# Sequence 0's lead-in in one block, and the third layer's three norms inside its mix: a four-layer transformer on one core

## The reference, cut to what matters

```python
xln = _ln(x, ln1_w, ln1_b)                 # x is already layer 3's normed input here
att_out = sigmoid(xln @ Wr) * (xln @ Wv) @ Wo
rwkv_state = xln @ Ws
x = x + att_out
h = _ln(x, ln2_w, ln2_b)                   # routed on, further down
```

## Time and profile before

| | us |
|---|---|
| median of 3 runs (2219.67, 2219.96, 2226.17) | 2219.96 |
| the profiled execution, as timed | 2215.92 |
| its span, first to last instruction | 2214.2 |
| first attention scores begin, from the span's start | 50.58 |
| layer 3, first norm of ffn to the start of norm 3b | 1578.14 to 1634.32 |
| `chunk_inputs3`, first projection to last spill | 1681.6 to 1817.8 |

### The profile page before, as it was taken

One profiled execution on the slowest core, in us unless ns is written; L12 is line 12 of the kernel. 1 busy time (PEld: TensorE's weight loads), 2 busy tenths in 40 slices (PEclk: granted clock), 3 DMA queues, 4 the chain that ended last, 5 costly groups with the idle time before them and its releaser, 6 DMA issues. The chain is left out here.

```text
span 2214.2 us, 45686 instructions
## 1 busy us (share of the span) xinstructions
PE 1846.9 (83%) x17745; PEld 992.8 (45%) x17751; DVE 1612.4 (73%) x2720; ACT 1216.6 (55%) x2472; POOL 674.7 (30%) x755
## 2 busy tenths in 40 slices
PE   2888877866647999999988889999788979887987
PEld 1222221443221335963233357776564434555755
DVE  5999999785779997569963955554756649876367
ACT  2999999532333886258866245556433620221475
POOL 1112120321675542124444633330214620000160
PEclk7899899987876999999989989999789979998986
DMA  8422430100551532733321122212001341430310
GB/s 280 91 58 58 97 77 1 77 19 6 136 190 30 123 59 79 209 76 68 50 32 45 43 65 66 65 53 80 11 23 46 123 142 75 141 94 13 119 53 34
DMA packets 156703, 171.87 MB, mean 78 GB/s; under 512 B 55468, under 2 KB 125174, under 8 KB 156482
## 3 DMA queue, kind: packets, MB, share of 16 engines
q1 hardware_dynamic: 142904, 144.03, 23.8%
q0 software_dynamic: 13584, 24.92, 4.5%
HBM read 95.58 MB, written 77.28 MB: 78 GB/s over the span
## 5 line engine op out<-in xcount | busy, mean ns | idle before, releaser
L464 ACT ACTIVATE a_E<-a_scores,a_nmax 128x512 f32<-128x512 f32 x512 | 343.2, 814 | 14.2 <-DVE a_nmax L397 13.2
L1057 ACT ACTIVATE a_E<-a_scores 128x512 f32<-128x512 f32 x512 | 273.8, 601 | 97.2 <-PE a_scores L1092 92.1
L397 DVE TENSOR_REDUCE a_nmax<-a_scores 128x2 f32<-128x1024 f32 x256 | 302.5, 1217 | 20.8 <-PE a_scores L479 17.1
L961 DVE TENSOR_REDUCE a_nmax<-a_first 128x2 f32<-128x1024 f32 x256 | 295.6, 1217 | 15.2 <-PE a_first L1082 14.0
L479 PE MATMUL a_scores<-a_Vh,a_Kh 48*128 48x512 bf16 x512 | 108.2, 421 | 96.0 <-ACT a_E L464 71.9
L1082 PE MATMUL a_first<-a_Kh,a_Qh 48*128 48x512 bf16 x512 | 148.2, 417 | 36.8 <-PEq L51 20.1
L492 PE MATMUL a_turn<-a_E,a_QS 128*32 128x256 f32 x2048 | 174.1, 417 | 2.3 <-DVE a_QS L407 1.8
L464 ACT ACTIVATION_READ_ACCUMULATOR a_E<-a_scores,a_nmax 128x1 f32 x512 | 167.0, 334 | 0.0
L1092 PE MATMUL a_scores<-a_Qh,a_Kh 51*128 51x512 bf16 x512 | 161.0, 396 | 5.1 <-PEq L51 1.9
L1114 PE MATMUL a_out<-a_E,a_V 128*32 128x256 f32 x2048 | 162.7, 398 | 0.0
L2193 POOL DMA_INDIRECT outs<-f_ye,f_row_at x80 | 78.2, 977 | 144.7 <-ACT f_ye L2314 112.5
(11 more groups left out here) (599 smaller groups left out, 4422.6 us busy)
## 6 DMA issues: line engine op xcount, KB each, us to landing
f_up<-in_L_up SPq DMA_DIRECT2D x32, 256.0 KB, 3.3
a_Kh<-a_rows_k SPq DMA_DIRECT2D x16, 384.0 KB, 6.5
a_Vh<-a_rows_v SPq DMA_DIRECT2D x16, 384.0 KB, 9.9
a_Qh<-a_rows_q SPq DMA_DIRECT2D x32, 192.0 KB, 4.9
a_Kh<-a_rows_k SPq DMA_DIRECT2D x32, 192.0 KB, 5.7
slots<-empty SPq DMA_DIRECT2D x8, 645.0 KB, 6.4
f_xe<-slots SPq DMA_DIRECT2D x40, 129.0 KB, 2.1
outs<-zeros SPq DMA_DIRECT2D x8, 512.0 KB, 4.7
```

Of the source, the lines that this page charges most:

```text
L397: v.tensor_reduce(nmax[:, rd % 2, r1, :, q], bank(b, u)[:], AX.X, ALU.max, negate=True).then_inc(S["max_ready"], 1)
L464: m = a.activation(E[:, u % NE, x], bank(b, u)[:, x], ACT.Exp, bias=nmax[:, rd % 2, r1, x, q:q + 1], accum_out=Z[:, rd % 2, r1, x, q:q + 1])
L961: v.tensor_reduce(out, slot_bank(n)[:], AX.X, ALU.max, negate=True).then_inc(S["slot_read"], 1)
L1057: a.activation(E[:, u % NE, x], ps_s[n % 3][:], ACT.Exp, scale=SCALE).then_inc(S["exp_ready"], 1)
```

## The change

Five things. (1) The loading block, `layer_norm` "0" and the first block of `attention0` become one block. x comes in five parts (the first is one sequence); sequence 0 alone is normed, turned, projected and split; the other sequences' norms and turns follow. ACT asks for the seven small weights at its very start. K and V are handled apart, in halves of 512 columns; ACT makes all three casts. SP writes K's parts, ACT V's; the rows are read back in eight smaller DMAs per tensor half, those of the first head group first (`load_first_rows`), and the first units wait only for these. (2) Sequence 1's K|V stays in f32; POOL makes its parts at the start of the attention block. (3) The twelve fills, `ln_cols` and the weights of ffn 0 are asked for inside the attention block, after the row loads of sequences 1 to 6. `QS` is zeroed by POOL in the first block, and the Exp table is loaded there. (4) In `ffn3`, norms 3 and 3a are merged into the mix: both roots come from the spreads of X, DVE and POOL each normalise four row groups per sequence (four for `rows`, four for XN), PE turns both; `ps_s`, `ps_o` and the two turning banks are one bank each. (5) In `chunk_inputs3`, ACT takes v's sigmoid after the gate, and POOL puts out two tiles ahead of the wait for it instead of one ahead and one behind.

The diff, cut to its core:

```diff
+def load_first_rows(eng, rows, dst, sem, first):
+
+    for x in range(2):
+        src = rows.rearrange("(x q i d) t s -> x (d t) q i s", x=2, q=2, d=HD)[x]
+        heads = dst[64 * x:64 * x + HD * TERMS].rearrange("p (q i) s -> p q i s", q=2)
+        for q in range(2):
+            if first:
+                eng.dma_start(heads[:, q, 0], src[:, q, 0]).then_inc(sem, 16)
+            else:
+                eng.dma_start(heads[:, q, 1:4], src[:, q, 1:4]).then_inc(sem, 16)
...
+                    load_x(0)
+                    sp.dma_start(g.ident[:], w["identity"]).then_inc(S["ident_loaded"], 16)
+                    for n in range(1, 5):
+                        load_x(n)
+                    sp.wait_ge(S["k_parts"], 1)
+                    spill_left(sp, rows_k[0], parts[:, :, 0:T], S["k_spilled"])
+                    sp.wait_ge(S["k_spilled"], NSP // 2)
+                    load_first_rows(sp, rows_k[0], Kh[:, 0], rows_first[0], True)
+                    sp.wait_ge(S["v_spilled"], NSP // 2)
+                    load_first_rows(sp, rows_v[0], Vh[:, 0], rows_first[1], True)
+                    load_first_rows(sp, rows_k[0], Kh[:, 0], rows_rest[0], False)
+                    load_first_rows(sp, rows_v[0], Vh[:, 0], rows_rest[1], False)
...
+                    pe.wait_ge(S["ident_loaded"], 16)
+                    turn(0)
                     pe.wait_ge(g.a0_loaded, 7 * 16)
...
+                    project(0)
+                    turn(1)
+                    turn(2)
+                    project(1)
+                    for b in range(3, NB):
+                        turn(b)
...
+                    statistics(0)
+                    variances(0, 0, 1)
+                    roots(0, 0, 1)
+                    normalise(0, R)
+                    for b in range(1, EARLY):
+                        statistics(b)
+                    variances(1, 1, EARLY)
                     v.wait_ge(g.a0_loaded, 7 * 16)
                     v.tensor_scalar(temp_bk[:], bkv[:, 0], temp[:], None, ALU.mult)
-                    add_bias(0)
-                    for b in range(FIRST):
-                        second(b)
-                        if b + 1 < FIRST:
-                            add_bias(b + 1)
-                        third(b)
+                    roots(1, 1, EARLY)
+                    v.wait_ge(S["k_made"], 1)
+                    take_k(v, ps[0][:, 0]).then_inc(S["k_ready"], 1)
+                    v.wait_ge(S["v_made"], 1)
+                    take_v(v, ps[0][:, 1]).then_inc(S["v_ready"], 1)
+                    v.drain()
+                    remainder(0, KV, 0, "first_cast", "second_rest")
+                    remainder(1, KV, 0, "first_cast", "second_rest")
+                    v.drain()
+                    remainder(0, rest, 1, "second_cast", "third_rest")
+                    remainder(1, rest, 1, "second_cast", "third_rest")
+                    for b in range(EARLY, NB):
+                        statistics(b)
+                    variances(2, EARLY, NB)
+                    for b in range(1, EARLY):
+                        normalise(b, 2)
+                    roots(2, EARLY, NB)
+                    for b in range(EARLY, NB):
+                        normalise(b, R - 1)
+                    v.wait_ge(S["k_made"], 2)
+                    take_k(v, ps[1][:, 0])
+                    v.wait_ge(S["v_made"], 2)
+                    take_v(v, ps[1][:, 1])
+
+                @block.gpsimd
+                def _(pool):
+                    pool.memset(QS[:], 0.0)
+                    for b in range(1, NB):
+                        pool.wait_ge(S["rstd_ready"], 2 if b < EARLY else 3)
+                        for r in range(2 if b < EARLY else R - 1, R):
+                            n, s = divmod(b * R + r, 2)
+                            m = pool.tensor_scalar(g.XN[:, b, r], g.X[:, b, r], stats[:, n, s, 1:2], rstd[:, n, s:s + 1],
+                                                   ALU.subtract, ALU.mult)
+                        m.then_inc(S["last_ready"], 1)
+                    pool.wait_ge(S["last_ready"], NB - 1)
...
+                    a.dma_start(Wk[:], w["L0_attn_Wk"]).then_inc(g.a0_loaded, 16)
+                    a.dma_start(Wv[:], w["L0_attn_Wv"]).then_inc(g.a0_loaded, 16)
+                    a.dma_start(bkv[:, 0], w["L0_attn_bk"].unsqueeze(0).broadcast_to([128, C])).then_inc(g.a0_loaded, 16)
+                    a.dma_start(temp[:], w["L0_temp_rows"]).then_inc(g.a0_loaded, 16)
+                    a.dma_start(bkv[:, 1], w["L0_attn_bv"].unsqueeze(0).broadcast_to([128, C])).then_inc(g.a0_loaded, 16)
+                    a.dma_start(Wq[:], w["L0_attn_Wq"]).then_inc(g.a0_loaded, 16)
+                    a.dma_start(bq[:], w["L0_attn_bq"].unsqueeze(1)).then_inc(g.a0_loaded, 16)
+                    a.wait_ge(S["zeroed"], 1)
+                    a.activation(g.unit_root[:], zeros[:, 0:1], ACT.Sqrt)
+                    root(0, 0, 1)
+                    taken(0)
+                    root(1, 1, EARLY)
...
+                    cast(0, 0, KV, "k_ready", "first_cast")
+                    cast(1, 0, KV, "v_ready", "first_cast")
+                    cast(0, 1, rest, "second_rest", "second_cast")
+                    cast(1, 1, rest, "second_rest", "second_cast")
+                    cast(0, 2, rest, "third_rest", "k_parts")
+                    cast(1, 2, rest, "third_rest", "v_parts")
+                    a.wait_ge(S["v_parts"], 1)
+                    spill_right(a, rows_v[0], parts[:, :, T:2 * T], S["v_spilled"])
+                    query(0)
+                    root(2, EARLY, NB)
+                    a.activation(spare[:], g.ident[:, 0:1], ACT.Exp)
+                    taken(1)
+                    taken(2)
+                    taken(3)
+                    query(1)
+                    for b in range(4, NB):
+                        taken(b)
...
-                sp.wait_ge(rows_sem[0], 64)
+                for n in range(2):
+                    sp.wait_ge(rows_rest[n], 64)
                 for b in range(1, NB):
                     n = b - FIRST + 1
-                    if n > 0:
-                        sp.wait_ge(S["parts_ready"], n)
+                    sp.wait_ge(S["parts_ready"], b)
                     spill_left(sp, rows_k[b], parts[:, :, 0:T], S["spilled"])
                     spill_right(sp, rows_v[b], parts[:, :, T:2 * T], S["spilled"])
                     sp.wait_ge(S["spilled"], b * NSP)
                     if n > 0:
                         sp.wait_ge(S["scores_ready"], (b - 1) * NU)
                     load(sp, b, b % 2)
+                    beside(sp, b)
...
-                v.memset(QS[:], 0.0)
-                v.drain()
...
-                        pe.wait_ge(rows_sem[s], (b - s) * 32 + 64)
+                    if b == 0 and u in (0, 8):
+                        for n in range(2):
+                            pe.wait_ge((rows_first if u == 0 else rows_rest)[n], 64)
+                    if b and u == 0:
+                        pe.wait_ge(rows_sem[s], (b + s) // 2 * 64)
...
-            layer_norm(nc, g, "3", g.X, g.XN, g.XT, ahead=load_weights, again=True)
-            g.recycle_sems()
-            layer_norm(nc, g, "3a", g.XN, rows, HT, scale=ln_cols[:, 0:1], bias=ln_cols[:, 1:2], by_row=True)
...
+            ps_s, ps_o, ps_h, ps_x = (km.ps(f"f3_ps_{n}", [128, T]) for n in ("s", "o", "h_turn", "x_turn"))
...
+                        if b + 1 < NB:
+                            turn_rows(b + 1)
                         inputs(b)
+                        turn_x(b)
                         if b:
...
+                        if b + 1 < NB:
+                            rows_turned(b + 1)
...
+                        a.wait_ge(S["x_turned"], b + 1)
+                        a.activation(g.XT[:, b].rearrange("c (p r) -> c p r", r=R), ps_x[:].rearrange("c (r p) -> c p r", r=R),
+                                     ACT.Identity).then_inc(S["x_ready"], 1)
...
+                @block.gpsimd
+                def _(pool):
+                    pool.wait_ge(S["rstd_ready"], 1)
+                    for b in range(NB):
+                        normalise(pool, 1, rows, b, R - 1).then_inc(S["last_row"], 1)
+                        for r in range(1, R):
+                            m = normalise(pool, 0, g.XN, b, r)
+                        m.then_inc(S["xn_rest"], 1)
+                    pool.wait_ge(S["xn_rest"], NB)
...
+                    def rows_out(b):
+                        for r in range(R - 1):
+                            m = normalise(v, 1, rows, b, r)
+                        m.then_inc(S["rows_ready"], 1)
+                        normalise(v, 0, g.XN, b, 0).then_inc(S["xn_first"], 1)
...
+                    v.tensor_scalar(var[:, 0], spreads, 1.0 / C, EPS, ALU.mult, ALU.add)
+                    v.tensor_scalar(var[:, 1], spreads, (1.0 + EPS) / C, EPS * EPS, ALU.mult, ALU.add
+                                    ).then_inc(S["var_ready"], 1)
+                    v.wait_ge(S["std_ready"], 1)
```

(28 more changed lines are left out.)

294 lines of the change are left out of this document (155 added, 139 removed).

## The result

| | us |
|---|---|
| kernel before, 20 executions beside the changed kernel | 2223.78 median (2214.75 to 2236.91) |
| changed kernel, 20 executions | 2208.33 median (2187.12 to 2229.89) |
| ratio, with its 95% interval | 0.9915 (0.9893 to 0.9936) |
| profiled execution of the changed kernel, as timed | 2219.57 |
| its span | 2217.8 |

What follows compares the result with a forecast made beforehand. No engine bounds the whole; late row DMAs hold the start, ACT the attention, PE the mix. Gains 16 + 9 + 1.5 = 26.5 us off 2215.9 give 2189.4, plus 4.0 for the median: 2193, range 2183 to 2206.

Steps and rivals of the forecast that it cites:

- the start: Joined first block: first scores at about 34.5 us instead of 50.6, gain 16 us, ends 19 and 12.
- ACT's asks: Start: seven DMA asks ahead of ACT's table load, 0.5 us each, ending at 4.2 us.
- PE's clock: Start, second projection: 4.5 us at the low clock, so 3.3 us of projection become 5.5.
- The collision of DVE and POOL: Start: DVE's four remainders wait for POOL's normalises, 0 to 0.83 us each, taken as 1.5 in all.
- Whatever start is saved there is kept: Attention after the start: ACT is the bound, so the start's saving, forecast at 16 us, stays.
- rival D: Layer 3's mix stays at clock 0.50: period 8.7 us, norm 3b 23 us later, total 2229.5; chance 0.04.
- The mix: Layer 3's ffn, norms merged into the mix: PE-bound period 4.5 us, gain 9 us, ends 4 and 11.
- Rival B: Layer 3's mix becomes DVE-bound at 5.3 us per sequence: 6.5 us less gain, total 2200; chance 0.12.
- v's sigmoid: chunk_inputs3: PE gets back at most its 3.1 us wait for squares; gain 1.5 us, ends 4 and -1.
- part 3: The chunk_inputs3 edits: v's sigmoid later, POOL's second tile ahead of the product; forecast gain 1.5 us.
- PE's unnamed 8.5 us may move either way: chunk_inputs3, inside the quads: PE's 8.5 us of waits without a named cause could grow or shrink.
- rival A: The start keeps less: serial ACT chain or low clock, scores at 42, 8 us less, total 2201; chance 0.14.

Runs made afterwards that it cites:

- e3: Kernel before with only the chunk_inputs3 edits (v's sigmoid later, POOL's tiles two by two): 2226.28 us, ratio 1.0020.
- e6: Changed kernel with eight full products added on PE ahead of layer 1's routing: 2190.35 us, ratio 0.9858.
- e8: Changed kernel with ACT's new order in chunk_inputs3 but POOL's old one (a tile, the product, a tile): 2213.28 us, ratio 0.9926.
- e10: Changed kernel with the hidden products of layer 1's routing made 128 columns wide instead of 64: 2207.44 us, ratio 0.9931.
- e2: Kernel before with only the norms merged into layer 3's mix: 2213.12 us, ratio 0.9953.
- e1: Kernel before with only the joined start, fills and loads moved into the attention: 2225.92 us, ratio 1.0012.
- e7: Changed kernel with vk's 512 KB spill asked for behind the next sequence's quads: 2195.51 us, ratio 0.9867.
- e12: Changed kernel with vk's spill late, first projection not waiting for bq, twelve full products added ahead of layer 1's routing: 2194.12 us, ratio 0.9870.

## Why the prediction was right, and where it wasn't

**Direction and mechanism of the start: right.** Gain 14.6 at the first scores and 15.7 at the end of attention 0 for 16 forecast, the block's start as releaser, a DMA share of 0.34 from 10 to 15 us, attention not longer (343.1 us of exponentials, has 343.2). Inside the sum several terms were off and partly cancel. The loads' landing: the sum has a term for ACT's asks (0.42 to 0.48 each, as assumed, and one of 1.34) and none for the time from ask to landing. That was 8.4 us for bq, and since all seven loads share one semaphore the first projection began at 12.81, 2.2 us after XT was there. PE's clock: the first projections ran at the low level too (2.07 for 1.1), which I had allowed only for the second. The level is read from the duration, which is that of 26.19 at a granted clock of 0.50; the clock's own record says 1.00 from 12 to 18 us, and the two don't agree there. With these V's parts came at 20.85 for 17.5, and K's at 20.2, outside the 15 to 17 that were to show the forecast right. The collision of DVE and POOL hardly arose: POOL's normalises ended at 18.02, and the four remainders (17.42 to 20.2) took 0.70 and 0.65 each, for 0.65 forecast and 1.5 in all for collisions. The turns and copies behind the second projection took 4.0 us (31.43 to 35.45) for 5.5, and the next block began 0.5 us behind them for 1.0. (The POOL cast of 1.04 us that the forecast compares with is the next sequence's, not the one two sequences on.)

**The sum's step that failed: "Whatever start is saved there is kept".** The sum takes it for the whole kernel. It was kept in attention 0 and ffn 0, and then an unchanged stage lost 20.2 of it. Every cost was looked for in the code that changes or stands beside it. The low clock was priced at the places where the change makes PE idle (rival D put it in the mix, where it did not come), and not in an unchanged stage that can run at either clock. Rows of before gave a warning that I didn't read: the routing begins behind 12.4 us of idle PE, and part of it runs at 0.50 before too.

**The mix: right.** 10.0 us for 9, period 4.35 for 4.5, PE the bound at clock 1. Eight turns cost 0.88, the lower end. The first inputs ran at the low clock to 1595.25, 11.2 us after the variance where 10.8 were forecast. Rival B (DVE-bound) and D fell.

**v's sigmoid: wrong sign.** The ends of the term were a gain of 4 and a loss of 1, and PE was to wait under 1 us for the squares in total. It waited 2.3 for 3.1 before, so 0.8 us came back. The spacing of q's spills in the kernel before was also read too favourably: one of the seven was 18.2, not 14.4 to 15. Over the profiled executions the stage takes 171.1 us without part 3 (six kernels, 168.1 to 174.5) and 176.1 with it (changed, e3, e6, e8, e10; 170.6 to 178.0): 5.0 us lost between two groups that overlap (e6 has 170.6 with part 3, e2 has 174.5 without). What I wrote down as "PE's unnamed 8.5 us may move either way" was the term that mattered. PE's pauses ahead of the projection, squares and unnamed together, rose by 2.1 (7.7 us in six sequences of before, 9.8 after): the squares' 1.8 went and 3.9 came without a name. In the third and the fourth sequence the one took the other's place; in the second nothing was waited for before, so taking away a wait isn't the whole cause. The larger part is the clock behind them. Counting each projection's excess over 3.69, it costs 1.4 us per execution without part 3 and 5.1 with it, 3.7 of the 5.0. Why one pause is followed by the low clock and another of the same length isn't stays open: e2 had pauses of 1.92 and 2.02 us and e1 one of 2.45, and the projection behind took 3.69.

**The total.** 15.7 and 10.0 were there, and -5.0 came for +1.5. That makes 20.7 where the routing is not long and nothing where it is. The measured gain, 15.5 by the medians of all executions and 18.9 by the ratio that leaves three out, lies nearer the upper end, so fewer of the unprofiled executions have the long routing than the four of seven profiled ones, or it costs them less; for e1 alone the account would give 15.8 or -4.4, and its ratio says that most had the loss. The executions without a profile carry only a mean clock (0.898 to 0.914 for the changed kernel, the low ones among the longest), so how often each takes the long routing stays open, and so does what gives the fastest ones 27.6. That the total by the ratio, 2201.1, lies inside the range is partly luck: it is the value of rival A, whose reason (scores at 42) didn't come, and it came from a stage that no term of the sum holds.

**Versions that beat both.** The changed kernel with vk's spill late (e7) has 0.9867 for 0.9915, and e6 and e12 are as good within their intervals. By what its profile explains, e7 is the one to keep: one request moved, 9.5 us less in its stage than the mean with part 3 and 4.5 less than the mean without.

## What to carry to other kernels

When an edit shifts later work in time, look in the trace for stages behind it that run partly at PE's low clock; they can take either of two lengths, and the gain must be judged over many executions, with the clock of that stage read in each profile. A wait that an edit removes may stand in front of another one, here that for instructions: before taking it out, ask what the engine will run into next, and count waits with and without a name together. Ask for large spills where the engine beside them runs few long instructions, not where it runs hundreds of short ones.
